# Where four score tiles stand among the transposed scores of a step: 32-wide attentions of a two-layer decoder on one core

## What is computed

```
B (L0 xattn): softmax(q k^T / 4) v, q from x (512 rows), k and v from the context (1024 rows)
D (L1 attn):  the same within x, with rope on q and k, causal mask (512 x 512)
E (L1 xattn): as B with biases and a mask over 512 x 1024
```

## Time and profile before

| | |
|---|---|
| median of 3 runs | 4661.04 us |
| lowest, highest | 4655.22, 4662.46 us |
| profiled execution | 4669.31 us |
| its span, first to last instruction | 4667.4 us |
| mean granted TensorE clock | 0.911 |
| busy: TensorE, VectorE, ScalarE | 3925.1, 2494.0, 1681.8 us |

### The profile page before, as it was taken

How to read it: one execution, slowest core, us unless ns; L and a number is a source line. 1 busy time by engine, 2 the same in 40 slices (tenths; PEclk the granted TensorE clock), 3 DMA queues, 4 the chain that set the end, 5 groups by cost and what they waited for, 6 DMA issues and landing times.

```text
span 4667.4 us, 57227 instructions
## 1 busy us (share of the span) xinstructions
PE 3925.1 (84%) x22002; PEld 1860.8 (40%) x22082; DVE 2494.0 (53%) x5948; ACT 1681.8 (36%) x2506; POOL 201.1 (4%) x219
## 2 busy tenths in 40 slices
PE   6777878899877878899977788889997779778998
PEld 2342334345334233435533424343553342433355
DVE  4466655732355765573235576557323657655632
ACT  2544423421254442352126354225113625422510
POOL 1000030000000003000000000200000000020000
PEclk9898988999989888899988898889998889988999
DMA  5213012122411202202241210230214130023031
GB/s 188 82 40 73 16 43 64 23 85 71 128 61 47 57 16 60 65 5 92 64 152 42 63 37 16 60 69 1 98 58 152 42 75 25 16 60 69 1 105 56
DMA packets 124718, 288.95 MB, mean 62 GB/s; under 512 B 12517, under 2 KB 74981, under 8 KB 115173
## 3 DMA queue, kind: packets, MB, share of 16 engines
q1 hardware_dynamic: 124424, 285.06, 21.0%
HBM read 206.37 MB, written 78.64 MB: 61 GB/s over the span
## 4 chain that ended last, share of the span: by engine, by line
PE 63%; DVE 17%; ACT 8%; DMA 5%; issue 3%; POOL 2%; SPq 1%; DVEq 0%; POOLq 0%; ACTq 0%
PE ps L1064 10%; PE ps L525 7%; PE ps L508 5%; PE ps L1082 5%; DVE mx L660 5%; PE ps L453 5%; PE ps L1385 3%; DVE ps L657 3%; ACT a_X L1454 3%; PE ps L339 2%; PE ps L1303 2%; DMA qparts<-QP 2%; PE ps L407 2%; PE ps L513 2%; DMA QS<-qparts 2%
## 5 line engine op out<-in xcount | busy, mean ns | idle before, releaser
L599 ACT ACTIVATE PT<-ps 128x1024 f32<-128x1024 f32 (+3 forms) x640 | 604.8, 959 | 477.0 <-PE ps L513 239.7
L453 PE MATMUL ps<-KS,QS 96*128 96x512 bf16 (+3 forms) x1280 | 481.8, 417 | 163.1 <-DMA QS<-qparts 63.3
L660 DVE TENSOR_REDUCE mx<-ps 128x1 f32<-128x512 f32 (+3 forms) x768 | 438.1, 619 | 225.7 <-PE ps L453 138.0
L1064 PE MATMUL ps<-xnT,f_w 128*128 128x512 f32 x1088 | 490.6, 594 | 0.0
L508 PE MATMUL ps<-QS,KS 99*128 99x512 bf16 (+2 forms) x1280 | 429.7, 381 | 10.4 <-ACT QS L589 6.2
L657 DVE CUSTOM_DVE_ANT_0 ps<-ps,mneg 128x512 f32<-128x512 f32 x512 | 342.4, 714 | 156.9 <-PE ps L453 154.8
L525 PE MATMUL ps<-PT,VP 128*32 128x512 f32 (+3 forms) x2560 | 385.0, 586 | 1.6
L1162 DVE TENSOR_TENSOR f_tm<-f_si,ps 128x512 f32<-128x512 f32 x128 | 88.0, 687 | 505.9 <-ACT f_si L1114 505.8
L453 PEld LDWEIGHTS ps<-KS,QS 96*128 96x128 bf16 x1280 | 130.8, 103 | 476.8 <-DVE mx L660 198.5
L1114 ACT ACTIVATE f_si<-ps 128x512 f32<-128x512 f32 x136 | 80.8, 597 | 610.3 <-PE ps L1077 591.2
L1064 PEld LDWEIGHTS ps<-xnT,f_w 128*128 128x128 f32 x1088 | 207.4, 191 | 205.1 <-issue 198.2
(11 more groups left out here) (244 smaller groups left out, 5624.2 us busy)
## 6 DMA issues: line engine op xcount, KB each, us to landing
f_w<-in_wF SPq DMA_DIRECT2D x136, 384.0 KB, 3.1
QS<-qparts SPq DMA_DIRECT2D x24, 768.0 KB, 5.9
scores<-a_fin SPq DMA_DIRECT2D x64, 256.0 KB, 3.1
a_fin<-scores SPq DMA_DIRECT2D x16, 1024.0 KB, 8.3
a_Y<-in_wA SPq DMA_DIRECT2D x5, 3072.0 KB, 14.7
scores<-a_fin SPq DMA_DIRECT2D x64, 192.0 KB, 2.9
a_fin<-scores SPq DMA_DIRECT2D x16, 768.0 KB, 4.3
a_fin<-scores SPq DMA_DIRECT2D x24, 512.0 KB, 3.7
```

The source lines that it names most:

```text
L453: last = nc.tensor.matmul(o, m["QS"][0:KR, h, i * P:(i + 1) * P], m["KS"][0:KR, h, f:f + w], start=True, stop=not c.causal)
L599: nc.scalar.activation(m["PT"][:, mp % 2, j % 2, :, 0:w], ps[:, b0:b0 + 2, 0:w], ACT.Exp, scale=HD ** -0.5).then_inc(g("exp"), 1)
L660: nc.vector.tensor_reduce(m["mx"][:, h % 2, i, f // BANK:f // BANK + 1], ps[:, k % 2, 0:w], AX.X, ALU.max, negate=True).then_inc(g("slot_f ...
L1064: last = nc.tensor.matmul(ps[:, 2 * v + e % 2, :], m["w"][:, e % NRING, (2 * v + k) * P:(2 * v + k + 1) * P], xnT[:, k, :], start=(k == 0) ...
```

## The change

Within a step the first score tile now stands ahead of `scores_t(t, 0)`, one stands behind it, and the rest follow `scores_t(t, 1)`. If the step's first slot is no tile (`den`), nothing is put ahead, and that slot alone stands between the two.

```diff
             for t in range(c.steps):
+                first, end = c.slots_to[t], c.slots_to[t + 1]
+                one = first + (first < end and c.slots[first][0] == "s")
+                two = min(one + 1, end)
+                fill(first, one)
                 scores_t(t, 0)
-                mid = (c.slots_to[t] + c.slots_to[t + 1]) // 2
-                fill(c.slots_to[t], mid)
+                fill(one, two)
                 if t:
                     for h in c.rows_after(t):
                         max_row(h)
                 if len(c.pairs_at(t)) == 2:
                     scores_t(t, 1)
-                fill(mid, c.slots_to[t + 1])
+                fill(two, end)
                 if t:
                     weighted(t - 1)
```

## The result

The changed kernel takes 4631.6 us (median of 4, 4627.8 to 4634.9), the kernel before 4659.5 in the same comparison: ratio 0.9935, 95% interval 0.9923 to 0.9947, so 25 to 36 us less. The forecast was 4638, 23 less than before, with a range of 4616 to 4653. The profiled execution has a span of 4632.9 us against 4667.4.

A forecast was written before the change was run, and what follows sets the result against it. No engine is full; a step in B is a loop of latencies between TensorE and VectorE. Four batches of B -4.0, E -2.2 and D +0.4 make -23.2 us, taking the median 4661.0 to 4638; range 4616 to 4653.

The forecast's parts named there:

- The loop: Stage B plain step: a tile issued first takes the first transposed scores out of the latency loop; 3.53 to 3.14 us.
- R steps of B: Stage B steps with a max row: VectorE's chain comes late and takes the gain; 3.59 to 3.63 us, 0.04 more.
- Den, norm and the lone den slot: Den steps 0.4 more in B, 0.43 in E; norm 0.32 less in B; lone den 0.4 more in B, D.
- the step behind: Stage B, step right after a norm slot: TensorE alone counts; 3.25 us against 3.53, twice, 0.6 less per batch.
- the first step without tiles: Stage E, after the tiles run out: delayed 0.4 us by VectorE's last chain.
- E was under-sized: Stage E's total per batch: 2.2 us less, from plain steps minus den and tail costs.
- The plain step: Stage E step without max row or den/norm slot: becomes TensorE-bound, 4.08 to about 3.76 us; 0.32 less x 11.
- R steps: Stage E steps with a max row: no wait in them, so 4.19 us stays; 0.
- the first two steps of each stage: Openings of B, D and E, at the lower clock: taken as 0, bounds -0.4 and +0.4 us each.
- The clock: TensorE's granted clock: neither gives nor takes in the sum; full level in B's steady steps despite waits.
- Rival 2: Starts of B, D, E: denser opening raises the clock one step sooner; 17 us more saved, 4621; chance 0.08.
- The sign that I named wrongly: Score tiles' line: TensorE's waits for VectorE should fall by over 20 us.

The follow-up runs named there:

- two-ahead: Against den-middle: two score tiles before the first transposed scores, none between the two transposed scores, two after; 4617.4 us, ratio 0.9911 to before.
- three-behind: Against den-middle: one score tile before the first transposed scores, none between, three behind the second; 4748.1 us, ratio 1.0194 to before.
- den-middle: Changed kernel with steps opening with a den slot, or holding only a den or norm slot, split as before; 4615.9 us, ratio 0.9914; again 4624.1 us.
- den bunch alone: Kernel before with only the new handling of steps not opening with a tile; 4693.6 us, ratio 1.0086; again 4692.0 us, ratio 1.0072.
- one, two, one: Against den-middle: one score tile before the first transposed scores, two between, one behind the second; 4638.7 us, ratio 0.9952 to before.
- late-row: Against den-middle: max row moved behind the second transposed scores; 4626.3 us, ratio 0.9930 to before; again 4623.9 us.
- stage-by-stage: Against den-middle: own tile order in B and D, max row late in D and E or in E alone; 4617.8 and 4614.6 us.

## Why the prediction was right, and where it was off

**The loop.** Right. X1 stood between two readings of VectorE and left the loop with a tile ahead of it: 3.14 as walked in B, ten times a batch. The two-ahead kernel (3.09 us in B with bunches) and the three-behind kernel (+92 us over before, in the expected range) tell this from "an even spread pays"; in E the spread has a share of 0.14 us a plain step.

**R steps of B.** 3.59 instead of 3.63, unchanged from before; 0.3 us a batch.

**Den, norm and the lone den slot.** Right: +0.37 twice in B and +0.41 twice in E (0.40 and 0.43), norm 0.32 less, the step behind 0.27 less, lone den +0.50 in B (0.4), +0.46 in D (0.4; before 2.85 us, after 3.31). In E the lone den, which the sum left out, cost 0.15, and the first step without tiles 0.37 more (0.4). Putting the den steps back gave 10.5 us.

**E was under-sized**: -2.2 a batch in the sum, -4.2 measured (160.96 to 156.72 us in the first batch). The plain step is 3.72, not 3.76: I kept the 0.14 us between T4 and W, and it is 0.09 when T4 has not waited. R steps lost 0.05, where I had 0. The largest single part is the step of the sum that said "the first two steps of each stage ... I take 0". They gave 0.74 in E (first tile to first W: 27.49 to 26.76) and 0.58 in B (25.36 to 24.79). And steps 2 and 3 still have one X, so less work for TensorE; there step 3, an R step costed at 0, gave 0.43 (4.18 to 3.75), and step 2 also 0.43. Together: 0.74 + 0.43 + 0.05 x 7 + 0.5 for the eleven plain steps beyond their 0.32 = 2.0 us, about what was missing. B has the same gap for the same reason, 0.58 a batch.

**The clock.** In the two profiled executions it played little part: the mean is 0.911 before and 0.910 after. (the earlier trace rows show the lower level at the start of B alone; the trace has it at those of D and E too, 0.50 from 696 to 710 us and from 812 to 836.) Rival 2 came in part all the same. B's second period of W tells whether the clock has risen (3.5 to 3.6 us, and 4.6 and more where it has not): in before's trace it had in one batch of four, in the changed kernel's in one of four (4.84 and 3.53 us in the second batch), in its repetition in all four, worth 1.3 to 2.2 us each. Over all traces it had risen by then in 9 of 16 B's with one leading tile (changed and den-middle), and in 2 of 12 in the old order (before and den bunch alone). That the sum could leave the clock out was thus in part the luck of the two traces. What I had not thought of is that den slots put the clock at risk in the middle of a stage; in the changed kernel B lost nothing by it in the first trace and 1.5 us in one batch of the second (5.89 and 5.79 us for 5.67 and 4.56).

**The sign that I named wrongly.** I forecast TensorE's waits at the tiles down by 20 us; they rose by 85 (58.0 at one maximum, 26.5 at the other). That row adds the idle time of the weight loads, which rose by 104 us; that a lone tile's load waits for its bank while matmuls go on is my reading of it. For the matmuls alone the forecast was nearly met: 89.1 to 69.6, 19.5 us less. The waits of the engine on the other side, VectorE, fell by 59.2 us (154.8 + 138.0 to 121.3 + 112.3). I also gave about 0.3 for VectorE's idle time before T1; my own walk, continued by one step, gives 0.60 (four tiles read by 2.96, next T1 there at 3.56), and 0.60 was measured.

## What to carry to other kernels

Where two engines pass work back and forth through two buffers, write down the loop of starts and see which instructions stand in it: moving one of them behind an issue that the other engine is waiting for pays by its full length (0.39 of X1's 0.44 us in B); spreading work evenly added nothing to that in B and 0.14 us a step in E, and as one, two, one it cost. Look at the rare steps separately: the rule that was right for the ordinary steps cost 10 us in the few that open with something else. Count the openings too, since a stage's first steps may lack the second half that makes the others bound by something else.

## What was not expected of the hardware

TensorE's granted clock fell to its lower level in the middle of dense attention stages. In the 14 traces of this study all such falls in B and D lie in a den step (4-column matmuls, with waits around them) or in the norm step behind it, and E, with the same slots, has none. One costs 1.0 to 1.6 us in the norm step (4.73 to 6.07, 4.89 to 6.40), and up to 4.2 us with the steps on either side (a norm step of 7.83 in place of 4.56). In D the place of the max row changed it (74.4 against 70.7 us, four batches of four). With the order fixed it can differ from batch to batch (B: 133.6 to 139.0 us in one trace).

It does not look like plain chance there: it goes with the moment at which the clock rose at the stage's start. In the 36 B's of the changed, den-middle, two-ahead, late-row and stage-by-stage kernels, all nine whose first period of W was 4.00 us or less (an early rise) had a fall in a den or norm step, and one of the 27 others did. With the den bunch alone the clock fell in the B with the one early rise (first period 4.30 us) and in the three whose second period was 4.67 to 4.83 us, and stayed up in the four with 5.01 to 5.09; three B's of before, at 4.64 to 4.81 but without the bunch, kept it. So the bunch and the moment of the rise both count, and an early rise can be paid for later in the stage. The pattern was found in the traces afterwards, and what links the two was not tested.

The den bunch alone cost 10 us by its steps and 34 to 37 us in time. In stage D it was there before the change, unseen by me: there the second den slot is followed by a W of 1.87 us, a step of 6.07 between W's instead of 4.73, in all four batches (6.02 to 6.29 us), and likewise after the change. Two stretches of before's trace, around the first den slot and around the second:

```profile
727.00:738.00 11.00, 9.97 (x88) 5.72 (x88) 7.54 (x25) 6.10 (x10) 0.00 (x0) 1.00 0.01 1
738.00:749.00 11.00, 10.23 (x77) 4.33 (x76) 7.31 (x24) 5.09 (x9) 0.00 (x0) 0.85 0.00 0
```

That the clock explains all of the den bunch's excess was not shown: 4.5 us of it can be read in B of the second trace, and stage C's 9.6 us go with a lower clock there.
